# Fills of the sorted array issued one step earlier, and four result buffers in the sorted stage

## The reference

```
x = x + L0_conv(ln(x))     # neighbourhood attention, 7 x 7, 12 heads of 16
t = t + L0_ffn(ln(t))      # 32 experts of 464, top 6, capacity 48, and a shared expert of 928
x = x + L1_conv(ln(x))     # attention inside one row of an image, 12 heads
t = t + L1_ffn(ln(t))      # causal attention over an image (12 heads, 3 key heads),
                           # then 16 experts of 384, top 2, no capacity
```

## Time and profile before

| | us |
|---|---|
| median of 3 runs | 1165.16 (1165.14 to 1166.06) |
| the profiled execution | 1164.46 |
| its span, first to last instruction | 1162.5 |
| PE busy | 990.2 (85%) |
| DVE busy | 689.5 (59%) |
| ACT busy | 525.4 (45%) |
| POOL busy | 319.5 (27%) |
| mean granted TensorE clock | 0.962 of full speed |
| DMA, bytes moved | 144.04 MB, 124 GB/s over the span |

### The profile page before, as it was taken

One profiled execution on the slowest core, in us unless ns is written; L12 is line 12 of the kernel. 1 busy time (PEld: TensorE's weight loads), 2 busy tenths in 40 slices (PEclk: granted clock), 3 DMA queues, 4 the chain that ended last, 5 costly groups with the idle time before them and its releaser, 6 DMA issues.

```text
span 1162.5 us, 25677 instructions
## 1 busy us (share of the span) xinstructions
PE 990.2 (85%) x9376; PEld 780.5 (67%) x9398; DVE 689.5 (59%) x2181; ACT 525.4 (45%) x1287; POOL 319.5 (27%) x514
## 2 busy tenths in 40 slices
PE   4799999999999879987879888889887769999991
PEld 2576776767767535565757676767766548989991
DVE  5686776866867423436466777776776564423334
ACT  0553634525436212204566767666667654222220
POOL 0000000000000083346544446474420221423331
PEclk9999999999999889998989999999998988999996
DMA  9150541513505499920000000000000029799935
GB/s 340 48 155 1 154 113 40 153 52 102 153 0 153 134 302 416 412 56 1 2 1 2 1 1 20 1 20 15 6 20 1 21 89 371 268 388 311 313 139 180
DMA packets 68852, 144.04 MB, mean 124 GB/s; under 512 B 4864, under 2 KB 55184, under 8 KB 66592
## 3 DMA queue, kind: packets, MB, share of 16 engines
q1 hardware_dynamic: 64208, 132.23, 33.9%
q0 software_dynamic: 4560, 10.69, 2.7%
HBM read 96.69 MB, written 46.20 MB: 123 GB/s over the span
## 4 chain that ended last, share of the span: by engine, by line
PE 48%; issue 17%; DVE 17%; ACT 8%; DMA 5%; POOL 4%; POOLq 0%; DVEq 0%; ACTq 0%; SPq 0%
PE bank L1919 8%; PE bank L644 5%; PE bank L667 4%; PE bank L2056 4%; DMA R<-in_ffn_gu 4%; DVE neg_max L745 3%; PE bank L709 3%; PE bank L598 3%; ACT R L774 3%; PE bank L1947 2%; PE bank L621 2%; PE bank L851 2%; ACT R L783 2%; PE bank L844 2%; DVE R L914 1%
## 5 line engine op out<-in xcount | busy, mean ns | idle before, releaser
L774 ACT ACTIVATE R<-bank,neg_max 128x128 f32<-128x128 f32 (+2 forms) x576 | 189.1, 401 | 85.4 <-DVE neg_max L745 84.0
L1095 POOL TENSOR_SCALAR R<-cf,ids_rel 128x128 bf16<-128x128 f32 x256 | 166.1, 667 | 39.4 <-PE bank L2036 38.8
L745 DVE TENSOR_REDUCE neg_max<-bank 128x2 f32<-128x352 f32 (+2 forms) x216 | 130.1, 610 | 57.9 <-PE bank L621 53.2
L644 PE MATMUL bank<-cf,R 128*128 128x128 f32 x864 | 136.5, 282 | 19.4 <-ACT R L783 14.8
L1047 POOL TENSOR_TENSOR rstd<-mean_var,cf 128x2 f32<-128x2 f32 x24 | 4.7, 196 | 447.0 <-DVE mean_var L909 447.0
L644 PEld LDWEIGHTS bank<-cf,R 128*128 128x128 f32 x864 | 98.0, 144 | 41.4 <-ACT R L774 22.1
L783 ACT ACTIVATE R<-bank 128x512 f32<-128x512 f32 (+1 forms) x216 | 102.6, 507 | 26.8 <-PE bank L644 26.8
L1919 PE MATMUL bank<-R 64*116 64x256 f32 (+1 forms) x512 | 97.7, 399 | 0.0
L797 ACT ACTIVATE R<-bank 128x1024 bf16<-128x1024 bf16 x72 | 71.2, 1021 | 53.9 <-PE bank L598 53.0
L598 PE MATMUL bank<-cb,R 128*128 128x128 bf16 x1008 | 71.1, 231 | 15.3 <-DVE R L575 15.3
L1919 PEld LDWEIGHTS bank<-R 64*116 64x116 f32 (+1 forms) x512 | 65.2, 180 | 26.4 <-issue 16.7
(11 more groups left out here) (257 smaller groups left out, 1842.6 us busy)
## 6 DMA issues: line engine op xcount, KB each, us to landing
R<-in_ffn_w SPq DMA_DIRECT2D x48, 864.0 KB, 7.3
sorted_x<-cmp SPq DMA_DIRECT2D x8, 4128.0 KB, 17.2
R<-in_ffn_gu SPq DMA_DIRECT2D x16, 1392.0 KB, 21.3
R<-in_ffn_dn SPq DMA_DIRECT2D x16, 768.0 KB, 18.5
xs_words<-sorted_x SPq DMA_DIRECT2D x47, 129.0 KB, 5.4
R<-token_y SPq DMA_DIRECT2D x8, 384.0 KB, 6.1
rows<-R SPq DMA_DIRECT2D x8, 224.0 KB, 2.3
out_x<-x_all SPq DMA_DIRECT2D x16, 96.0 KB, 2.4
```

What stands on the lines that cost most here:

```text
L644: ins = nc.tensor.transpose(PT[u % 2][:, at + g * P:at + (g + 1) * P], probs[:, u % 3, g * kw + c0:g * kw + c0 + P], ident)
L745: nc.vector.tensor_reduce(neg_max[:, u % 4, 0:g], score_bank(a, u)[:, 0:g * kw].rearrange("p (g k) -> p g k", g=g), AX, ALU.max, negate=Tr ...
L774: ins = nc.scalar.activation(probs[:, u % 3, g * kw:(g + 1) * kw], score_bank(a, u)[:, g * kw:(g + 1) * kw], ACT.Exp, bias=neg_max[:, u % ...
L1095: ins = nc.gpsimd.tensor_scalar(comb_s[i % 2][:, t, j, :], cst("iota_tok"), ids_rel[:, j:j + 1], None, ALU.is_equal)
```

## The change

In SP's list the fill of image i goes ahead of the wait for image i's rows (`a_row`), so it is issued behind the row store of image i - 1, and the first one in the start-up. In the sorted stage `y_f` and `place_i` have four buffers (tile modulo 4), `f_stored` has four semaphores, and the wait ahead of line 1853 is for the scatter of four tiles ago. POOL's loop takes four tiles a turn. `token_y` gets two more blocks for rows without a token, and the constants that point there are widened. Three semaphores are merged into others: `e_empty` into `set` (which now counts to 2), `b_idf` into `b_link` (to 3), `f_link` into `f_place` (two counts a tile).

```diff
-            sp.wait_ge(s("set"), 1)
+            sp.wait_ge(s("set"), 2)
             sp.dma_start(sx[NBLOCK - 1], empty).then_inc(s("zeroed"), 16)
             with sp.Fori(0, B) as i:
+                sp.dma_start(sz[bass.ds(i, 1)].rearrange("a p n c -> (a p) n c"),
+                             empty.unsqueeze(1).to_broadcast([P, E1 * REG // B, ROW1])).then_inc(s("zeroed"), 16)
                 sp.wait_ge(s("a_row"), i + 1)
                 sp.dma_start(rows0_t[bass.ds(i, 1), :, :, :].rearrange("a p t c -> (a p) t c"), row0)\
                     .then_inc(s("row_stored"), 16)
-                sp.dma_start(sz[bass.ds(i, 1)].rearrange("a p n c -> (a p) n c"),
-                             empty.unsqueeze(1).to_broadcast([P, E1 * REG // B, ROW1])).then_inc(s("zeroed"), 16)
...
-            for r in range(2):
-                sp.wait_ge(s(f"f_stored{r}"), 16 * ((TILES + 1 - r) // 2))
+            for r in range(4):
+                sp.wait_ge(s(f"f_stored{r}"), 16 * ((TILES + 3 - r) // 4))
...
-            pool.wait_ge(s("b_idf"), 1)
+            pool.wait_ge(s("b_link"), 3)
...
-            def f_body(n, tiles):
-                for r in range(tiles):
-                    t = 2 * n + r
+            def f_body(n, r0, r1):
+                for r in range(r0, r1):
+                    t = 4 * n + r
                     pool.wait_ge(s("f_yc"), t + 3)
...
-            f_body(0, 2)
+            f_body(0, 0, 2)
             c_scatter(B - 1)
-            with pool.Fori(1, TILES // 2) as n:
-                f_body(n, 2)
-            f_body(TILES // 2, TILES % 2)
+            f_body(0, 2, 4)
+            with pool.Fori(1, TILES // 4) as n:
+                f_body(n, 0, 4)
+            f_body(TILES // 4, 0, TILES % 4)
...
                     for r in range(tiles):
-                        if not first or j:
-                            dve.wait_ge(s(f"f_stored{r}"), 16 * (n * (TURN // 2) + j // 2))
-                        dve.wait_ge(s("f_place"), t + r + 1)
-                        nc.vector.tensor_tensor(place_i[:, r:r + 1], places[:, (j + r) % WRING:(j + r) % WRING + 1],
-                                                cst("limit")[:, r:r + 1], ALU.min)
+                        q = (j + r) % 4
+                        if not first or j >= 4:
+                            dve.wait_ge(s(f"f_stored{q}"), 16 * (n * (TURN // 4) + j // 4))
+                        dve.wait_ge(s("f_place"), 2 * (t + r) + 2)
+                        nc.vector.tensor_tensor(place_i[:, q:q + 1], places[:, (j + r) % WRING:(j + r) % WRING + 1],
+                                                cst("limit")[:, q:q + 1], ALU.min)
                     dve.wait_ge(s("f_y"), t + tiles)
-                    nc.vector.tensor_copy(y_f[:, 0:tiles, :], two(M0[:, 0:2 * C])[:, 0:tiles, :])\
+                    nc.vector.tensor_copy(y_f[:, j % 4:j % 4 + tiles, :], two(M0[:, 0:2 * C])[:, 0:tiles, :])\
                         .then_inc(s("f_yc"), tiles)
```

More of the change, by code:

```diff
@@ L82 @@
 NCF = _lay(CF, [("ident", P), ("iota_slot", CAP), ("iota_tok", P), ("cos", 2 * HD), ("sin", 2 * HD),
-                ("tiles", 16), ("sorted", NSORT), ("half", 2), ("neg", 6), ("back", 1), ("place", NT + 2), ("experts", E1), ("spread", P), ("regions", E1), ("limit", 2), ("upto", E1 * E1)])
+                ("tiles", 16), ("sorted", NSORT), ("half", 2), ("neg", 6), ("back", 1), ("place", NT + 4), ("experts", E1), ("spread", P), ("regions", E1), ("limit", 4), ("upto", E1 * E1)])
 NCB = _lay(CB, [("identb", P), ("tri", P), ("ones", P), ("lies", 4 * HD), ("sees_n", 4 * HD), ("sees_w", 4 * HD),
@@ L108, in constants @@
     put(f, CF, "back", -P)
-    put(f, CF, "place", np.arange(NT + 2)[None, :] * P + p[:, None])
+    put(f, CF, "place", np.arange(NT + 4)[None, :] * P + p[:, None])
     put(f, CF, "experts", 1 + np.arange(E1))
     put(f, CF, "regions", TOK * np.arange(E1))
-    put(f, CF, "limit", 2 * TOK + np.arange(2)[None, :] * P + p[:, None])
+    put(f, CF, "limit", 2 * TOK + np.arange(4)[None, :] * P + p[:, None])
     e = np.arange(E1)
@@ L373, in build @@
         wsl = sb("wsl", [P, NPAIR])
-        y_f = sb("y_f", [P, 2, C])
+        y_f = sb("y_f", [P, 4, C])
         counts = sb("counts", [P, 6, E1])
@@ L387, in build @@
         empty = cmp2[:, :, :].rearrange("p a b -> p (a b)")[:, 0:ROW1]
-        place_i = sb("place_i", [P, 2], I32)
+        place_i = sb("place_i", [P, 4], I32)
         second = sb("second", [P, WRING])
@@ L412, in build @@
         sorted_x = nc.dram_tensor("sorted_x", [(NBLOCK + 4) * P, ROW1], F32)
-        token_y = nc.dram_tensor("token_y", [2 * TOK + 2 * P, C], F32)
+        token_y = nc.dram_tensor("token_y", [2 * TOK + 4 * P, C], F32)
         rows0_t = rows0[:, :].rearrange("(i t p) c -> i p t c", t=2, p=P)
@@ L1009, in rows_ahead @@
             def rows_ahead(t, j):
-                load_rows(t + WRING, j, lambda: (sp.wait_ge(s("f_xT"), t + 1), sp.wait_ge(s("f_place"), t + 1)))
+                load_rows(t + WRING, j, lambda: (sp.wait_ge(s("f_xT"), t + 1), sp.wait_ge(s("f_place"), 2 * t + 2)))
             sp.wait_ge(s("c_u"), nth_square("h", B - 1))
@@ L1341, in _ @@
                 nc.vector.tensor_scalar(m_row(b)[:, :, TOKC], cst("place")[:, 0:2], 2.0 * P * (b - 2), None, ALU.add)
-            nc.vector.memset(empty, 0.0).then_inc(s("e_empty"), 1)
-            dve.wait_ge(s("e_empty"), 1)
-            nc.vector.tensor_copy(empty[:, TOKC:TOKC + 1], cst("place")[:, NT + 1:NT + 2]).then_inc(s("set"), 1)
+            nc.vector.memset(empty, 0.0).then_inc(s("set"), 1)
+            dve.wait_ge(s("set"), 1)
+            nc.vector.tensor_copy(empty[:, TOKC:TOKC + 1], cst("place")[:, NT + 3:NT + 4]).then_inc(s("set"), 1)
             dve.wait_ge(s("wqkv_loaded"), 32)
@@ L1351, in _ @@
             link.end()
-            dve.wait_ge(s("set"), 1)
+            dve.wait_ge(s("set"), 2)
             nc.vector.memset(onehot[0][:, :, :], 0.0)
@@ L1452, in _ @@
             nc.vector.tensor_copy(ids_rel[:, :], ids_f[:, :])
-            nc.vector.tensor_copy(ids_i[:, :], ids_f[:, :]).then_inc(s("b_idf"), 1)
+            nc.vector.tensor_copy(ids_i[:, :], ids_f[:, :]).then_inc(s("b_link"), 1)
             dve.wait_ge(s("a_shared"), B)
@@ L1478, in b_body @@
                 dve.wait_ge(s("b_y"), jj + 1)
-                link(nc.vector.tensor_tensor(y_f[:, :, :], two(M1[:, 0:2 * C]),
+                link(nc.vector.tensor_tensor(y_f[:, 0:2, :], two(M1[:, 0:2 * C]),
                                              wsl[:, bass.ds(2 * jj, 2)].unsqueeze(2).to_broadcast([P, 2, C]), ALU.mult))
@@ L1484, in b_body @@
                 nc.vector.memset(scratch[:, 14:15], 0.0).then_inc(s("b_yc"), 1)
[L1485 to L1488, removed]
+                link(nc.vector.tensor_copy(part(0), y_f[:, 0:2, :]))
+                link(nc.vector.tensor_tensor(y_f[:, 0:2, :], y_f[:, 0:2, :], part(0), ALU.subtract))
+                link(nc.vector.tensor_copy(part(1), y_f[:, 0:2, :]))
+                link(nc.vector.tensor_tensor(part(2), y_f[:, 0:2, :], part(1), ALU.subtract))
                 link.end()
@@ L1813, in f_place @@
                 nc.vector.tensor_tensor(second[:, at], x[:, FIRST:FIRST + 1], tile_n[:, bass.ds(t, 1)], ALU.not_equal)\
-                    .then_inc(s("f_link"), 1)
-                dve.wait_ge(s("f_link"), t + 1)
+                    .then_inc(s("f_place"), 1)
+                dve.wait_ge(s("f_place"), 2 * t + 1)
                 nc.vector.scalar_tensor_tensor(places[:, at], second[:, at], float(TOK), x[:, TOKC:TOKC + 1],
@@ L1884, in _ @@
             conv_v_pe(pe, NEIGH, headT, wqkv, 0)
-            pe.wait_ge(s("set"), 1)
+            pe.wait_ge(s("set"), 2)
             transpose_qk(pe, NEIGH, 0)
```

6 lines of the change are left out of this document (3 added, 3 removed).

## The result

The changed kernel takes 1150.81 us in the median of 4 runs (1149.6 to 1155.78), the one before 1165.61 (4 runs). The ratio is 0.9874, with a 95% interval of 0.9837 to 0.9911. So 14.8 us were won of the 16.8 that were forecast, and the time is inside the forecast's range. Two more sets of runs of the same kernel, each against the kernel before on its own chip, gave 0.9899 (0.9875 to 0.9922) and 0.9873 (0.9844 to 0.9903), which is 11.8 us and 14.8 us.

What follows compares the result with a forecast made beforehand. Bounds: gathered rows behind the eighth fill at the turn; TensorE in the sorted stage, partly held by scatter waits. Gains 6.8 + 10.0 = 16.8 from 1164.46 gave 1147.7, or 1148.4 as median; range 1144.5 to 1154.5, 80 in 100 for the forecast case.

Steps and rivals of the forecast that it cites:

- The start-up and the merged semaphores: Start of the kernel: the first fill, issued early, and the merged semaphores cost 0; one waiting load at most 17.2 us.
- The earlier rows: Turn to the experts: gathered rows land 5.6 us after issue without the fill, so TensorE starts 3.5 us earlier (0 to 6.56).
- The clock: First expert matmuls after the turn: less idle time lowers TensorE's clock less, gaining 1.0 us (0 to 2.7).
- The later waits for weights: First experts: TensorE's two later waits for gate-and-up weights go, gaining 2.3 us (0 to 2.3).
- the turn and the experts: From images to first experts: earlier rows 3.5, clock 1.0 and weight waits 2.3, in sum 6.8 us.
- The sorted stage: Sorted tiles with four buffers: 8.4 between down projections, 0.5 for rows and 1.1 at the tail, in sum 10.0 us.
- between the down projections: Sorted stage: scatter waits go entirely, 16 pairs at 6.76 us take 108.2 instead of 116.57, gaining 8.4 us (4.9 to 8.4).
- the tail: End of the sorted stage: no scatter wait before the last copies, so POOL's last go comes 1.1 us earlier.
- the rows ahead: Start of the sorted stage: an earlier third copy shortens TensorE's wait for sorted rows by 0.5 us (0 to 0.8).
- The rows come no earlier: Rival at the turn: gathers meet weight loads and land as late; turn gives 2.3 alone, time 1152.9; 10 in 100.
- The wait changes its name: Rival in the sorted stage: TensorE waits for weights or sorted rows instead; gain 6.8 + 1.1, time 1157.3; 5 in 100.
- The slower case: More scatters in flight delay rows for every pair, 1174 at 1.2 us a pair (2 in 100), or first fill holds start-up (1).

Runs made afterwards that it cites:

- the kernel that holds both weights: Changed kernel, with SP holding pair 3's gate-and-up and down weight loads, and all behind them, until the first two gathers landed: 1148.8 us, ratio 0.9866.
- the holds: Changed kernel with pair 3's weight loads held until the first two gathers landed: both loads 1148.8 us; down weights only 1148.54 and 1147.91 us.
- the kernels that keep the order of rows and weights: All except two kernels with down weights held and sorted rows loaded before weights: tiles 12 and 13 (1150.18 us), tiles 12 to 15 (1149.67 us).

## Why the prediction was right, and where it was not

**The start-up and the merged semaphores: 0.** Right, by the twelve profiles. The 1.6 us by which the changed kernel's first profile starts earlier are chance, and luck for that set: the place is 67.4 and 69.1 in the old order of the fills and 67.4 to 70.1 in the new one.

**The earlier rows: 3.5 forecast, about 2 measured.** The step that was mis-sized is the landing of a gather beside weight loads. I took 5.6 us from the second's issue, the middle between scatters' median and their worst; it is 7.1 to 7.6, above the worst scatter of the earlier trace rows. It was 9.3 and 9.5 before (the bound that I called 9.1 is 9.3 by its own rows), so 2.0 us are gained. The nearest row by kind was the scatter under a saturated queue, 6.8, and I should have stayed at it: SP's two loads were issued right ahead of the gathers. What I had wrong is also the reason. I wrote that POOL's queue stood still only with the fill; it stands still with weights too, for 2.5 us instead of 4.5, and then shares the engines with a down load. The fit of the Trainium skill (DMA: Bandwidth & Descriptors, Anatomy of one DMA), 2.3 us for this size, is an estimate for one DMA and has no term for what runs beside it. With nothing in flight the gather took 3.4 us from the start of POOL's instruction to its use, and 2.4 from that instruction's end (0.96 us later), so the fit is right or 1 us short by where one counts from. With loads in flight it is short by 3 to 7 us.

**The clock: 1.0 forecast, none.** The idle time of 4.5 us was still enough: granted clock 0.59 and 0.50 from 410 to 420, and 3.36 us for the group in both kernels. In the four profiles with an idle time of 2.4 to 2.7 us it fell too (0.50 to 0.75 from 415 to 420), and the group took 3.23 to 3.36. With 0.7 it didn't fall (1.00 throughout, 1.78). From the first transpose to the first combine matmul, less the waits for weights, it is 91.5 and 91.3 us with the fill in its old place and 90.8 to 92.3 with it moved: nothing is gained there. So the two terms are one: the clock's part comes only with rows that are nearly in time., where 2.23 us of idle time brought it down, said the same: no gain. I took 1.0 in the middle all the same.

**The later waits for weights: 2.3 forecast.** They are gone in every profile with the fill moved, but for the kernel that holds both weights. But with the fill in its place they are 2.3 in one profile and 0.5 in another, so the term is worth 0.5 to 2.3.

Together the turn and the experts took 116.9 and 115.1 us with the fill in place, and 113.3, 113.8, 112.5, 114.0 and 111.9 with it moved: 2.9 us between the means (116.0 and 113.1), where 6.8 were forecast. These 3.9 us are the error, and more than the 2.0 by which the first set of times fell short. In its profile the earlier start hid 1.6 of them, and the turn's 3.6 came from a profile before with the larger wait for weights. The forecast was right in its range and in the sorted stage; for the turn it was right in direction and over twice too high.

**The sorted stage: 10.0 forecast, 10.0 measured** (162.6 and 162.9 with two buffers; 152.8, 153.0, 153.0, 152.1 and 153.1 with four). Its terms: between the down projections 116.57 became 108.53, 8.0 for 8.4, the rest being two new waits for sorted rows, 0.4 us in all; the tail 1.1 as forecast (the last go came 14.58 us earlier, the down projection of 1123.68 13.45); the rows ahead 0.65 for 0.5. The wait for the old scatter doesn't occur once, as the 4 us of spare time said. The lowered clock behind the longest wait went with the wait, so the upper end of that term, not 4.9, was the right one. The buffers alone, with the fills in the old order, gave the same (153.0), so this part is shown by its own run.

**The rivals.** "The rows come no earlier" is half true: its reason, weights instead of the fill, is what the holds showed, though 2 us remained. The Trainium skill's rule in DMA: Bandwidth & Descriptors, Queues, rings and completion order, that an engine goes round its queues packet by packet, fits the second part of the wait and not the first: both queues were served together for 4.7 us (0.33 and 0.77 MB), but in the 2.5 us before, POOL's queue moved nothing and SP's 0.97 MB. "The wait changes its name" happened at a twentieth to a seventh of its size: in the kernels that keep the order of rows and weights, the pairs behind SP's pause take 0 to 1.3 us more than 6.76 in all. The slower case didn't come up: scatters still leave at TensorE's pace.

## What to carry to other kernels

A bulk transfer with a late deadline should be issued where no one waits for a transfer behind or beside it, and its old place should be priced by what remains in flight there once it is gone: here two weight loads remained, and of the 6 us by which the gathers were later than with nothing in flight they kept 4. Where a small gather is on the critical path, try to hold the bulk load that is needed latest (here 768 KB, and what follows it) until the rows have landed; holding 1392 KB more made the stage behind wait 3.2 us. A buffer that is released by a scatter to DRAM can want more copies even if its wait is hidden most of the time: here VectorE's waits were 2.1 us in the mean and 5.1 at most in a period of 6.76, and four copies for two gave 10 us. Three were not tried.

The best version found is the changed kernel with the down weights of pair 3 held: 0.9843 of the kernel before in two sets, against 0.9873 of the changed kernel beside the second (intervals that overlap).

## What the runs showed of the hardware

The second gather of 128 rows by POOL was used 3.4 us after its issue with nothing in flight, after 5.1 to 5.4 with a 1392 KB load of SP ahead of it, 7.1 to 7.6 with a 768 KB load behind that one, and 9.3 to 9.5 with the rest of a fill ahead of both. POOL's queue moved nothing in the first 2.0, 2.5 and 4.5 us of these, while SP's moved 0.8 to 1.2 MB.

With the fill of 4128 KB on its queue, SP's next issue took 9.2 and 9.3 us, and 0.36 without it.

The granted clock from 415 to 420 was 0.50 to 0.58 after an idle time of TensorE of 4.4 to 6.8 us, 0.50 to 0.75 after 2.4 to 2.7 and 1.00 after 0.7.

Single executions of one program on one core spread from 1160.1 to 1169.9 us. The profiles differ most in stage C (468.6 to 471.7) and in the start (67.4 to 70.1), which the change doesn't touch or doesn't move. The turn and the experts differ by up to 2.1 us between profiles with the same order of loads, the sorted stage by up to 1.3.
